# A GpSimd gather loop of two tiles, with ids loaded a tile at a time

## The reference, cut to what matters

```python
e = jnp.stack([tbl_0[ids[:, 0]], ..., tbl_25[ids[:, 25]]], axis=1)
all_vecs = jnp.concatenate([dense_proj[:, None, :], e], axis=1)
interactions = jnp.einsum('bnd,bmd->bnm', all_vecs, all_vecs)
interact_flat = interactions[:, rows, cols]          # the upper triangle
z = jnp.concatenate([dense_proj, interact_flat], axis=1)
h = jnp.concatenate([z, r_dense_proj], axis=1)
h = jnp.maximum(h @ W_top1 + b_top1, 0.0)
h = jnp.maximum(h @ W_top2 + b_top2, 0.0)
y = h @ W_top3
```

## Time and profile before

| | us |
|---|---|
| median of 3 runs | 452.38 |
| lowest, highest | 450.32, 454.48 |
| the profiled execution: its time | 455.76 |
| the profiled execution: its span (first to last instruction) | 453.8 |
| PE busy in the span | 377.8 |
| POOL busy in the span | 231.0 |
| mean granted TensorE clock | 0.947 |

### The profile page before, as it was taken

One profiled execution on the slowest core, in us unless ns is written; L12 is line 12 of the kernel. 1 busy time (PEld: TensorE's weight loads), 2 busy tenths in 40 slices (PEclk: granted clock), 3 DMA queues, 4 the chain that ended last, 5 costly groups with the idle time before them and its releaser, 6 DMA issues.

```text
span 453.8 us, 14936 instructions
## 1 busy us (share of the span) xinstructions
PE 377.8 (83%) x6224; PEld 341.5 (75%) x6224; DVE 254.9 (56%) x767; ACT 146.3 (32%) x265; POOL 231.0 (51%) x244
## 2 busy tenths in 40 slices
PE   0769993968989799887998789887999788998877
PEld 0758893967887688876897689776998687886645
DVE  5997798663534865456555766456654765321110
ACT  2355130413313342333323342332413351335212
POOL 4365656465465454556555555555565535556000
PEclk9998996878996999999899999999998998999969
DMA  7999925151431314132341517151343411111000
GB/s 182 230 225 231 241 60 105 34 103 46 80 77 49 83 40 104 40 83 68 60 84 45 99 41 85 60 102 49 66 90 53 86 29 40 40 40 48 4 1 0
DMA packets 25441, 36.37 MB, mean 80 GB/s; under 512 B 5378, under 2 KB 19594, under 8 KB 25417
## 3 DMA queue, kind: packets, MB, share of 16 engines
q1 hardware_dynamic: 17577, 20.27, 24.6%
q0 software_dynamic: 7680, 15.74, 12.9%
q10 hardware_dynamic: 160, 0.01, 0.0%
HBM read 35.99 MB, written 0.01 MB: 79 GB/s over the span
## 4 chain that ended last, share of the span: by engine, by line
PE 69%; DVE 12%; issue 11%; DMA 3%; POOL 2%; ACT 1%; SPq 0%; DVEq 0%; ACTq 0%
PE hid L421 11%; DVE onehot L607 9%; PE look_ps L379 8%; PE look_ps L377 8%; PE gram L449 8%; PE look_odd L379 6%; PE hid L428 6%; PE look_odd L377 6%; PE vec_act L332 5%; POOL vecs L315 2%; DMA vecs<-tbl,ids_sb 2%; PE hid L377 2%; PE hid L379 2%; PE look_odd L374 2%; PE small L390 2%
## 5 line engine op out<-in xcount | busy, mean ns | idle before, releaser
L315 POOL DMA_INDIRECT vecs<-tbl,ids_sb x240 | 230.8, 962 | 187.0 <-issue 121.0
L607 DVE TENSOR_SCALAR onehot<-step_ids,row_no 125x256 fp32r<-125x256 int32 x704 | 210.6, 361 | 141.4 <-PE look_ps L379 49.0
L377 PE MATMUL look_ps<-onehot,look_hi 125*128 125x256 f32 x312 | 85.1, 305 | 7.8 <-DVE onehot L607 3.9
L580 ACT COPY vecs_T<-vec_act 128x512 f32<-128x512 f32 x64 | 37.6, 597 | 151.7 <-remote 67.3
L379 PE MATMUL look_ps<-onehot,look_lo 125*128 125x256 f32 x312 | 80.6, 291 | 1.6 <-issue 1.6
L449 PE MATMUL gram<-vecs_T 128*27 128x26 f32 x4096 | 50.3, 197 | 22.6 <-issue 22.5
L377 PEld LDWEIGHTS look_ps<-onehot,look_hi 125*128 125x128 f32 x312 | 62.2, 199 | 8.6 <-issue 8.1
L449 PEld LDWEIGHTS gram<-vecs_T 128*27 128x27 f32 x4096 | 43.9, 108 | 31.4 <-issue 28.1
L377 PE MATMUL look_odd<-onehot,look_hi 125*128 125x256 f32 x240 | 63.8, 300 | 1.9 <-issue 1.8
L379 PEld LDWEIGHTS look_ps<-onehot,look_lo 125*128 125x128 f32 x312 | 62.2, 199 | 3.4 <-issue 3.2
L379 PE MATMUL look_odd<-onehot,look_lo 125*128 125x256 f32 x240 | 60.1, 284 | 2.8 <-issue 2.7
(11 more groups left out here) (89 smaller groups left out, 325.7 us busy)
## 6 DMA issues: line engine op xcount, KB each, us to landing
step_ids<-look_ids SPq DMA_DIRECT2D x7, 768.0 KB
table_raw<-tbl SPq DMA_DIRECT2D x11, 448.0 KB
step_ids<-look_ids SPq DMA_DIRECT2D x7, 640.0 KB
vecs<-tbl,ids_sb POOLq DMA_INDIRECT x240
step_ids<-look_ids SPq DMA_DIRECT2D x11, 128.0 KB, 10.8
vecs<-dense SPq DMA_DIRECT2D x16, 64.0 KB
table_raw<-tbl SPq DMA_DIRECT2D x11, 52.0 KB
w_sb<-w SPq DMA_DIRECT2D x1, 512.0 KB
```

The source lines that it names most:

```text
L315: nc.gpsimd.indirect_dma_start(out=vecs[j][:, 1 + k, :], out_offset=None, in_=tables[k], in_offset=bass.IndirectOffsetOnAxis(ap=ids_sb[:, ...
L377: nc.tensor.matmul(bank, look_hi[:, f, ch, :], onehot[:, SLOT[g], c, :], start=ch == 0, stop=False)
L580: return engine_copy(vecs_T[j][:, :, 1 + lo:1 + hi], bank[:, 0:hi - lo, :].rearrange("d v b -> d b v"))
L607: last = nc.vector.tensor_scalar(onehot[:, SLOT[g], c, :], step_ids[a][0:LOOK_K, f - TABLES_OF[a][0], :], row_no[0:LOOK_K, ch:ch + 1], Non ...
```

## The change

`ids_sb` shrinks to two tiles' worth of ids (128 x 2 x 15). SP loads 7.5 KB of ids for each tile by itself (`load_ids`), 16 loads in all, with one semaphore for each of the two buffers. From tile 2 on such a load waits until PE has turned all of tile t-2, which is after all gathers of tile t-2 have read their ids. In SP's loop the two loads stand behind the dense loads. POOL waits for the tile's ids ahead of each tile's gathers, and runs tiles 2 to 15 in a loop of two tiles, with the waits' values in registers. The array of ids in memory is no longer transposed, so that one tile's ids are contiguous.

```diff
-        ids_sb = sb("ids_sb", [P, tiles, GATHERS], I32)
+        ids_sb = sb("ids_sb", [P, 2, GATHERS], I32)
...
-        ids_in = sem("ids_in")
+        ids_in = [sem(f"ids_in{j}") for j in range(2)]
...
+                def load_ids(t, j, pair):
+                    if positive(pair):
+                        sp.wait_ge(turned, GROUPS * (t - 1))
+                    sp.dma_start(ids_sb[:, j, :], ids[at(t), :]).then_inc(ids_in[j], 16)
...
                 load_first_ids(0)
-                sp.dma_start(ids_sb[:, :, :], ids).then_inc(ids_in, 16)
+                load_ids(0, 0, 0)
                 load_table(0)
                 load_first_ids(1)
                 load_table(1)
                 load_first_ids(2)
+                load_ids(1, 1, 0)
                 sp.dma_start(ident[:, :], identity).then_inc(ident_in, 16)
...
                 load_step(1, 1)
+                load_ids(2, 0, 1)
                 load_dense(2, 0)
                 load_dense(3, 1)
+                load_ids(3, 1, 1)
                 with sp.Fori(2, pairs) as r:
                     load_step(0, r)
                     load_step(1, r)
                     load_dense(2 * r, 0)
+                    load_ids(2 * r, 0, r)
                     load_dense(2 * r + 1, 1)
+                    load_ids(2 * r + 1, 1, r)
...
-                def gather(t):
-                    j = t % 2
-                    if t >= 2:
+                def gather(t, j, pair):
+                    opening = isinstance(pair, int) and pair == 0
+                    pool.wait_ge(ids_in[j], 16 * (pair + 1))
+                    if not opening:
                         pool.wait_ge(turned, GROUPS * (t - 1))
                         pool.wait_ge(gram_half0, t - 1)
                         pool.sem_inc(gather_begun, 1)
...
-                            in_offset=bass.IndirectOffsetOnAxis(ap=ids_sb[:, t, k:k + 1], axis=0),
+                            in_offset=bass.IndirectOffsetOnAxis(ap=ids_sb[:, j, k:k + 1], axis=0),
...
-                pool.wait_ge(ids_in, 16)
-                for t in range(tiles):
-                    gather(t)
+                gather(0, 0, 0)
+                gather(1, 1, 0)
+                with pool.Fori(1, pairs) as r:
+                    gather(2 * r, 0, r)
+                    gather(2 * r + 1, 1, r)
```

More of the change, by code:

```diff
@@ L308, in gather @@
                         half = k >= HALF_START[1]
-                        if k in HALF_START and t < 2 and t + k > 0:
+                        if k in HALF_START and opening and t + k > 0:
                             pool.wait_ge(onehot_used, FIRST_UNITS[2 * t + half])
                             pool.sem_inc(gather_begun, 1)
-                        if k == HALF_START[1] and t >= 2:
+                        if k == HALF_START[1] and not opening:
                             pool.wait_ge(gram_half1, t - 1)
@@ L865 @@
         "dense": dense,
-        "ids": np.ascontiguousarray(ids[:, large].reshape(-1, P, GATHERS).transpose(1, 0, 2)),
+        "ids": np.ascontiguousarray(ids[:, large]),
         "look_ids": np.ascontiguousarray(ids[:, small].T),
```

## The result

| | before | change |
|---|---|---|
| median of 20 runs each, us | 453.09 (447.96 to 459.37) | 459.24 (452.0 to 462.97) |
| ratio of the two, with its 95% interval | | 1.0097 (1.0053 to 1.014) |
| profiled execution, us (span) | 455.76 (453.8) | 458.93 (457.1) |
| granted clock, mean | 0.947 | 0.951 |

The account below looks back on a forecast made before the run. It took PE to bound the kernel (busy 83%, 69% of the chain), with POOL a supplier with room. Only the opening's -0.5 us counted, all else 0: 452.38 - 0.5 = 451.9 us, range 449 to 457.

Parts of the forecast that it names:

- Opening: Head of the load queue: 112.5 KB of ids no longer ahead of the tables; -0.5 us, bounds 0 and -0.6.
- Ids of tile 2: Load SP issues from 46.54: lands between 50.8 and 59.7, before tile 2's first gather at 60.90; cost 0.
- Ids in SP's loop: Later id loads land in time and delay the next `step_ids` by only 0.3 us; cost 0.
- POOL's added work: Waits, register work and branches in POOL's loop hide in its idle 3 us; cost 0, fully exposed 5.2 us.
- The small loads: DMA engines: 16 loads of 7.5 KB in 60-byte pieces, the same bytes as before; cost 0.
- The straight code goes: POOL's one 1.90 us gap inside a half may be code coming in, which a loop saves; value 0, bound -1.6.
- The first: Slower rival: gathers are on the path, so POOL's added work counts in full; 457.1 us, chance 0.12.
- The coincidence that spoke for this rival: Tile 8: ACT copies PE's 236.10 group only at 241.86, 1.67 us after POOL's last gather of that half ended.
- The jumps: Slower rival: POOL's seven loop jumps each stall 1.6 us on instruction refetch, 11.2 us, so 463 us; chance 0.04.
- The faster rival: Gathers on a hidden path, POOL's added work covered, and the single gap's 1.6 us saved: 450.3 us, chance 0.12.
- the late ids: Tile 2's first gather starts at 61 or 62 instead of 60.9, and PE waits longer: 453 to 454 us, chance 0.06.
- the tiles' period: In the loops: about 25.5 us per tile; any change in it would show the prediction wrong.

Follow-up runs that it names:

- e3: The kernel before with its one 120 KB load of ids split into three (tile 0, tile 1, the rest): 414.28 us, 0.9989 of the kernel before.
- f4: The change with each id load placed behind a `step_ids` load in SP's loop: 457.03 us, 1.0088 of the kernel before.
- g1: The change with POOL's gathers of tiles 2 to 15 written out instead of looped: 462.93 us, 1.0021 of the kernel before (462.04 us).
- g4: The change, unedited, run again where the kernel before took 462.04 us: 466.59 us, 1.0117 of the kernel before.
- e1: The change with POOL's gathers of tiles 2 to 15 written out instead of looped: 414.08 us, 1.0000 of the kernel before (413.77 us).
- g3: The kernel before plus twelve 7.5 KB loads into a spare buffer nobody reads, with one wait at the end of SP's program: 463.67 us, 0.9998.
- e2: The kernel before with POOL's gathers looped, later tiles using the ids of tiles 0 and 1: 413.74 us, 1.0007 of the kernel before (413.77 us).
- g2: The kernel before with POOL's gathers looped, later tiles using the ids of tiles 0 and 1: 465.24 us, 1.0068 of the kernel before (462.04 us).
- h3: The kernel before with POOL's gathers looped, later tiles using the ids of tiles 0 and 1: 454.30 us, 1.0013 of the kernel before (455.29 us).
- i1: The change without POOL's wait for ids in the loop; later ids go to a spare buffer and are not used: 458.9 us, 1.0166 of the kernel before.
- group g: Four kernels run on one chip with the kernel before (462.04 us), to test POOL's loop and the small loads apart and the whole change.
- group h: Four kernels run on one chip with the kernel before (455.29 us), to test the jump and repeated ids; the change gave 1.0118 there.
- f3: The change with `ids_sb` kept at its old size, so buffers behind it keep their old addresses: 459.98 us, 1.0188 of the kernel before.
- h2: The kernel before, POOL's code straight, but every later tile gathers by the ids of tiles 0 and 1: 454.59 us, 0.9996 of the kernel before.
- i2: The change with POOL's three waits reordered, the one for PE's products first: 458.19 us, 1.0138 of the kernel before.
- h1: The kernel before with POOL's gathers in seven one-turn loops, constants in the waits, ids of tiles 0 and 1 repeated: 455.39 us, 0.9991.

## Why the prediction was wrong

The forecast, no difference at 0.77, did not come; it is slower by about 1%, for which it had 0.15, and 459.24 is above the range's 457. By its steps:

1. *Opening, -0.5 us.* Right in mechanism: the table lands 1.2 us earlier, more than the 0.6 allowed. It is worth nothing that can be measured: e3, which does this part alone, gives 0.9989 with 0.4% to either side, and that holds the 0.5 us (0.1%) as well as zero. Nor do the traces that lose time keep the lead: tile 2's second half starts at 72.0 in them and at 71.0 in the others.
2. *Ids of tile 2, 0.* Right: POOL waits for ids at tile 0 alone.
3. *Ids in SP's loop, 0.* The load itself was in time everywhere. `step_ids` went 2.6 us behind it at pair 6, where I had priced 0.3 us (how much of that the ids made is not shown), and 21.9 us ahead of DVE's use (277.12 to 299.05). f4 puts them ahead and still costs 1.0088, so the queue's order isn't the cost.
4. *POOL's added work, 0 and at most 5.2.* **This is the step that failed**, in its size as in its reasoning: I put POOL's loop at nothing because its instructions stand in POOL's idle time, and looked for its price only in front of POOL's wait. The price there is indeed nil (1.55 and 1.56 us from products to gather). Yet the change costs 1.0097 to 1.0118 on four occasions, and without the loop 1.0021 in the group that has both (g1 against g4's 1.0117; e1's 1.0000 has no change beside it). So nearly all of the loss needs the loop, and it comes by a way that none of POOL's own rows shows.
5. *The small loads, 0.* Right by themselves: g3 gives 0.9998, e1 1.0000. What I did not price is loads and loop together. The loop alone cost 0.1% (e2), 0.7% (g2) and 0.1% (h3); with the loads and their waits on SP it costs 1.0 to 1.2%, and 1.7% where POOL doesn't wait for them (i1). In group g the two parts add up, 0.2 + 0.7 = 0.9 against 1.2, within the intervals; in group h the loop's 0.1% leaves 1.1% for what loads and loop do only together, if e1 and g1 hold there. Which of the two it is stays open.
6. *The straight code goes, 0 to -1.6.* The supposition behind it fell: the gap of 1.90 us inside a half stays at 1.91 with the loop. It isn't straight code coming in: every trace has it, ahead of the 114th gather, and in a loop of 30 gathers the 114th has no code of its own. What it is stays open.

**The rivals.** The first gave 457.1 us, nearer to what came than the forecast, but by its mechanism POOL would have to be later after its release, and it is not; the loop alone would have to cost most of the 5.2 us, and in h3 it costs 0.1%; and i1, which takes one of the four waits of each tile away, is no cheaper. A number that fits does not make a mechanism right. The coincidence that spoke for this rival was misread, too: the gathers that are over at 240.19 are tile 8's second half, while the group that PE turns at 236.10 is of its first half, whose last gather was over at 226.50 (225.56 + 0.94). The jumps don't stall: 40 to 53 ns each in the rows of L335. The Trainium skill, Runtime: NRT & Kernel Launch, section Instruction fetch mechanics, says that a taken branch whose target lies outside the loaded pages has to wait for a fetch. Whether POOL's loop reaches outside them no run shows; no jump in the trace has such a stall. The faster rival and the late ids did not come either.

**The signs.** Of the prediction's signs of being wrong one came: the tiles' period moved, from 25.8 to 26.1 us over tiles 2 to 15 in the means above. Of its signs of being right two failed: the 1.90 us gap is there, and PE waits for gathered vectors four times (6.8 us) and not at tile 2 alone.

**What is open.** The cause. A loop of POOL's, with small loads beside it, leaves PE idle for longer, while POOL's own starts follow PE as before; how, no run shows. Tried and excluded: the buffers' addresses (f3), the queue order on SP (f4), the loads' own traffic (g3), repeated ids (h2), POOL's wait for ids (i1) and the order of its waits (i2). Not separated: a loop with register waits but no jump, since h1 lost the register waits; the loads' waits on SP and the opening by themselves where the change costs; a loop with the loads but without their waits on SP; and the whole change where the kernel before takes 413.8 us. No version here beats the kernel before: e3, the nearest, gives 0.9989 (0.9945 to 1.0032).

## What to carry to other kernels

Rows that show an engine's added work hidden, and its reaction unchanged, bound what that engine adds to its own path; they don't bound what a rewritten program of it does to the rest. For such a rewrite keep a percent of the time as a possible price even where every step comes out at nothing, and test its parts together as well as alone: here the loads alone cost nothing that could be told and the loop alone 0.1 to 0.7%, but the whole 1.0 to 1.2%.

## What the runs showed of the hardware that I had not expected

The same kernel takes 413.8 us in one group and 451.8 to 462.0 us in the others, and the two kinds wait for different things. In the trace of e1 (413.8 us kind) no wait is put down to "remote", and PE waits for the gathered vectors instead:

```profile
PE vec_act L347 <- DMA vecs<-tbl,ids_sb: 22.8, 13, 8.2
```

In the slower kind it is the other way round: ACT's 67.3 us on "remote", PE's 22.5 us of gaps in the products, and only 7.6 us for vectors. e1 and g1 are the same program, and each ran on a chip numbered 0: 414.08 us (PE busy 362.5 us of a span of 410.2) and 462.93 us (385.1 of 460.9). If the number names one chip, it is not the chip but its condition that makes the 12%; what condition is not shown. The granted clock is only a little apart, 0.967 and 0.933 in these two profiles. A price measured in one kind need not hold in the other.

POOL's wait shows in the queue's records of some kernels and not of others (duration ns min/median/max). In g1, straight code with constants in its waits:

```profile
L319 POOLq EVENT_SEMAPHORE  x14: 43/43/43, 59.5 to 403.1; - x14
```

In the change, with registers in its waits:

```profile
L319 POOLq EVENT_SEMAPHORE  x14: 1477/9470/12981, 56.3 to 389.1; - x14
```

And in the kernel before, which is straight code with constants again:

```profile
L306 POOLq EVENT_SEMAPHORE  x14: 8273/9442/11333, 48.8 to 386.6; - x14
```

So a record of 9 us marks neither a loop nor waits on registers, as the expectation of i2 had taken it, and not the loss either: h2 has it (median 9460 ns) and loses nothing, i2 has none (its records in front of a tile take 17 ns) and costs 1.0138.
